# Two-expert routed layer: the routed experts' second product with the weights stationary, and three moves around it

## The reference, cut to what matters

```python
x = L0_attn_x                                   # (4, 1024, 128) float32
xn = _layernorm(x)
s = attention(xn)                               # 16 heads of 8, elu+1, rope, softmax, plus a 3-tap convolution of v
g = _silu(ffn(xn))
x = x + s * g

def ffn(u):
    h_s = experts_mlp(u, g_shared, W1_s, b1_s, W2_s, b2_s).sum(axis=-2)        # 2 shared experts, 128 -> 512 -> 128
    scores = jax.nn.sigmoid(u @ centroids)                                      # 8 routed experts
    gpk, i_topk = jax.lax.top_k(scores, 2)
    gk = gpk / scores.sum(axis=-1, keepdims=True)
    routed_all = experts_mlp(u, g_routed, W1_r, b1_r, W2_r, b2_r)
    h_r = (gk[..., None] * take(routed_all, i_topk)).sum(axis=-2)
    return u + h_s + h_r
# experts_mlp: gelu(rmsnorm(u) @ W1 + b1) @ W2 + b2
```

## Time and profile before

| | |
|---|---|
| median of 3 runs | 1197.69 us (1197.49 to 1198.04) |
| the profiled execution | 1197.96 us |
| its span, first to last instruction | 1195.8 us |
| mean granted TensorE clock | 0.983 |
| TensorE (PE) busy | 1151.4 us, 96% |
| TensorE weight loads (PEld) | 696.4 us, 58% |
| VectorE (DVE) busy | 832.6 us, 70% |
| ScalarE (ACT) busy | 753.3 us, 63% |
| GpSimd (POOL) busy | 393.0 us, 33% |

### The profile page before, as it was taken

How to read it: one execution, slowest core, us unless ns; L and a number is a source line. 1 busy time by engine, 2 the same in 40 slices (tenths; PEclk the granted TensorE clock), 3 DMA queues, 4 the chain that set the end, 5 groups by cost and what they waited for, 6 DMA issues and landing times.

```text
span 1195.8 us, 17687 instructions
## 1 busy us (share of the span) xinstructions
PE 1151.4 (96%) x6212; PEld 696.4 (58%) x6212; DVE 832.6 (70%) x1562; ACT 753.3 (63%) x1393; POOL 393.0 (33%) x436
## 2 busy tenths in 40 slices
PE   5999999799989999999999999999999999999996
PEld 4666679799965545555555555555555555545542
DVE  6723243255538888887888888788888878888870
ACT  5454455444546666766666667666666676766676
POOL 0166653300025371441506153251515234142000
PEclk9799999899999999999999999999999999999998
DMA  9011145554431202021120202112020202112000
GB/s 339 10 52 45 45 128 158 139 151 144 147 88 43 79 6 59 15 77 36 39 61 5 58 15 76 29 44 62 8 58 15 76 11 58 46 28 56 4 7 5
DMA packets 73864, 75.32 MB, mean 63 GB/s; under 512 B 25248, under 2 KB 58912, under 8 KB 73264
## 3 DMA queue, kind: packets, MB, share of 16 engines
q1 hardware_dynamic: 69680, 65.80, 20.0%
q0 software_dynamic: 4096, 8.40, 2.4%
HBM read 30.06 MB, written 18.35 MB: 40 GB/s over the span
## 4 chain that ended last, share of the span: by engine, by line
PE 63%; DVE 6%; issue 1%; ACT 0%; POOLq 0%; POOL 0%; DVEq 0%; ACTq 0%
PE ps L1431 22%; PE ps L1443 20%; PE ps L1088 18%; DVE neg_half L1155 4%; PE ps L1109 1%; DVE acc L1502 1%; PE ps L1117 1%; PE ps L1114 0%; DVE pre L1184 0%; PE ps L1102 0%; ACT prob L1471 0%; DVE pv_sb L1507 0%; DVE attn L1198 0%; DVE r_sum L1193 0%; ACT L1471 0%
## 5 line engine op out<-in xcount | busy, mean ns | idle before, releaser
L1155 DVE TENSOR_REDUCE neg_half<-ps 128x1 f32<-128x512 f32 x1024 | 647.2, 684 | 178.4 <-PE ps L1088 168.6
L1471 ACT ACTIVATE prob<-ps 128x512 f32<-128x512 f32 x1024 | 545.1, 598 | 210.9 <-PE ps L1431 190.6
L1431 PE MATMUL ps<-q_raw,k_mask 128*128 128x512 f32 x1024 | 431.4, 426 | 4.4 <-ACTq L1464 3.9
L1088 PE MATMUL ps<-k_raw,q_mask 128*128 128x512 f32 x1024 | 412.9, 403 | 9.1 <-DMA q_mask<-raw 6.3
L1431 PEld LDWEIGHTS ps<-q_raw,k_mask 128*128 128x128 f32 x1024 | 191.7, 188 | 231.8 <-ACT prob L1471 160.8
L1443 PE MATMUL ps<-prob,v_st 128*32 128x512 f32 x2048 | 272.7, 604 | 2.5 <-issue 1.2
L1088 PEld LDWEIGHTS ps<-k_raw,q_mask 128*128 128x128 f32 x1024 | 193.6, 189 | 50.7 <-DVE neg_half L1155 14.6
L629 ACT ACTIVATE hidden<-ps,w 128x512 f32<-128x512 f32 x92 | 62.9, 688 | 83.9 <-PE ps L513 77.5
L1385 POOL TENSOR_TENSOR result<-attn,acc 128x256 f32<-128x256 f32 x16 | 11.8, 736 | 294.6 <-DVE attn L1198 158.0
L534 PEld LDWEIGHTS ps<-w,hidden 128*128 128x128 f32 x736 | 95.4, 193 | 6.2
L534 PE MATMUL ps<-w,hidden 128*128 128x128 f32 x736 | 97.5, 276 | 0.0
(11 more groups left out here) (152 smaller groups left out, 1018.4 us busy)
## 6 DMA issues: line engine op xcount, KB each, us to landing
w<-in_w SPq DMA_DIRECT2D x23, 322.0 KB, 4.0
k_mask<-k_raw SPq DMA_DIRECT2D x64, 96.0 KB
slots<-zero SPq DMA_DIRECT2D x4, 1472.0 KB, 11.6
w_raw<-in_w SPq DMA_DIRECT2D x23, 256.0 KB, 2.9
x_tok<-slots SPq DMA_DIRECT2D x23, 256.0 KB, 3.3
answers<-y_tok SPq DMA_DIRECT2D x23, 256.0 KB, 2.3
k_raw<-raw SPq DMA_DIRECT2D x16, 256.0 KB
q_mask<-raw SPq DMA_DIRECT2D x64, 64.0 KB
```

Of the source, the lines that this page charges most:

```text
L1088: nc.tensor.matmul(max_bank(par, k, lone_bank)[:, :], q_mask[par][:, j, qt * P:(qt + 1) * P], k_raw[par][:, kh * CH:(kh + 1) * CH], start= ...
L1155: nc.vector.tensor_reduce(out=neg_half[par][:, qt, j, kh:kh + 1], in_=max_bank(par, k, lone_bank)[:, :], axis=AX.X, op=ALU.max, negate=True)\
L1431: nc.tensor.matmul(score_bank(n, par, s)[:, :], k_mask[par][:, j, kt * P:(kt + 1) * P], q_raw[par][:, qh * CH:(qh + 1) * CH], start=True, ...
L1471: nc.scalar.activation(prob[s // J % 2][:, j, :], score_bank(n, par, s)[:, :], ACT.Exp, scale=SCALE)\
```

## The change

The routed blocks' `down` takes the form of the shared ones: w2 stationary, the hidden tile moving, one product of 512 columns a step. Each routed block's sums are then copied by ScalarE (into the first four tiles of `xr_all`, free by then), transposed back by `stand` in step 3 of the next block, and taken by VectorE's `output`, which moves from step 2 to step 3. For the last block, copy, transposes and output come at the end of the stage. `FIRST_MAX` goes from 9 to 10. The two `y_tok` tiles become the halves of `x_b`, which is now reserved from the start; the wait for the last stores moves from the end of the stage to the third one, on SyncE ahead of the load of `x_b` and on GpSimd ahead of the first gather. ScalarE does one exponential of a single column at the end of the stage.

```diff
-        y_tok = [sb(f"y_tok{i}", [P, CT, C]) for i in range(SPARE)]
+        y_tok = ffn["y_tok"]
         b2_sum = sb("b2_sum", [P, C])
+        warm = sb("warm", [P, 1])
...
+        def lying_of(u):
+
+            return (lying if u < SHARED else ffn["xr_all"][:, 0:CT, :].rearrange("p t c -> p (t c)"))
...
                 ahead.sync(sp, k)
-            for i in range(SPARE):
-                sp.wait_ge(y_st[i], 16 * ((ROUTED + SPARE - 1 - i) // SPARE))
...
                 pe.wait_ge(gelu_ok, n + 1)
-                if u < SHARED:
-                    nc.tensor.matmul(bank[:, :], w2, hidden[n % HB][:, :], start=q == 0, stop=q == of(u) - 1)\
-                      .then_inc(down_ok, 1)
-                    return
-                for t in range(CT):
-                    last = nc.tensor.matmul(bank[:, t * P:(t + 1) * P], hidden[n % HB][:, t * P:(t + 1) * P], w2,
-                                            start=q == 0 and t == 0, stop=q == of(u) - 1, skip_group_check=True)
-                last.then_inc(down_ok, 1)
+                nc.tensor.matmul(bank[:, :], w2, hidden[n % HB][:, :], start=q == 0, stop=q == of(u) - 1)\
+                  .then_inc(down_ok, 1)
...
-                    if 1 <= u <= SHARED and q == LAG + 1:
+                    if 1 <= u and q == LAG + 1:
                         stand(u - 1)
...
+            stand(UNITS - 1)
...
+            def lay_down(u):
+                act.wait_ge(down_ok, hids_before(u + 1))
+                if u > 0:
+                    act.wait_ge(stood_full, u)
+                nc.scalar.activation(lying_of(u), y_ps[u % 2][:, :], ACT.Copy).then_inc(lying_ok, 1)
...
-                if 1 <= u <= SHARED and q == LAG:
-                    act.wait_ge(down_ok, hids_before(u))
-                    if u > 1:
-                        act.wait_ge(stood_full, u - 1)
-                    nc.scalar.activation(lying[:, :], y_ps[(u - 1) % 2][:, :], ACT.Copy).then_inc(lying_ok, 1)
+                if 1 <= u and q == LAG:
+                    lay_down(u - 1)
...
+            lay_down(UNITS - 1)
+            nc.scalar.activation(warm[:, :], ffn["gain_r"][:, :], ACT.Exp).then_inc(warm_ok, 1)
+            act.wait_ge(warm_ok, 1)
...
             def output(u):
-                if u < SHARED:
-                    dve.wait_ge(stood_full, u + 1)
-                else:
-                    dve.wait_ge(down_ok, hids_before(u + 1))
+                dve.wait_ge(stood_full, u + 1)
...
-                if q == (LAG if u > SHARED else LAG + 1) and u > 0:
+                if q == LAG + 1 and u > 0:
                     output(u - 1)
...
-        FIRST_MAX = 9
+        FIRST_MAX = 10
...
+        def answers_stored(eng):
+
+            for i in range(2):
+                eng.wait_ge(answer_st[i], 16 * ((ROUTED + 1 - i) // 2))
...
+            answers_stored(sp)
             sp.dma_start(x_b[:, :, :], x_v[0, :, :, :]).then_inc(x_b_in, 16)
...
                 if n == 0:
+                    answers_stored(pool)
                     gather(0, 0, KT * TOPK)
...
+            ffn["y_tok"] = [tiles["x_b"][:, i * CT:(i + 1) * CT, :] for i in range(2)]
+            ffn["y_st"] = tiles["answer_st"]
```

More of the change, by code:

```diff
@@ L376, in experts @@
         y_out = sem("f_y_out")
-        y_st = [sem(f"f_y_st{i}") for i in range(SPARE)]
+        y_st = ffn["y_st"]
         v_full = sem("f_v_full")
+        warm_ok = sem("f_warm_ok")
         rest_full = sem("f_rest_full")
@@ L541, in stand @@
                 for t in range(CT):
-                    last = nc.tensor.transpose(y_ps[u % 2][:, t * P:(t + 1) * P], lying[:, t * P:(t + 1) * P],
+                    last = nc.tensor.transpose(y_ps[u % 2][:, t * P:(t + 1) * P], lying_of(u)[:, t * P:(t + 1) * P],
                                                ident[:, :])
@@ L862, in attention @@
         neg_max = sb("neg_max", [P, KT, J, 1])
+        x_b = sb("x_b", [P, KT, C])
         s_ps = psum[0:SB]
@@ L867, in attention @@
         first_round_ps, first_max_ps = psum[6], psum[7]
+        answer_st = [sem(f"a_answer_st{i}") for i in range(2)]
         w_in = sem("a_w_in")
@@ L1282, in attention @@
         tiles = {"k_mask": k_mask[0], "q_mask": q_mask[0], "stage": stage, "rope": rope, "feat": feat, "pre": pre,
-                 "v_st": v_st}
+                 "v_st": v_st, "x_b": x_b, "answer_st": answer_st}
         first_stages(Ahead, tiles)
@@ L1294, in attention @@
         picked = [sb(f"picked{i}", [P, KT, C]) for i in range(TOPK)]
-        x_b = sb("x_b", [P, KT, C])
         tanh_b = sb("tanh_b", [P, KT, C])
```

## The result

| | before | after |
|---|---|---|
| median of 20 runs | 1197.49 us (1196.18 to 1198.08) | 1199.89 us (1198.37 to 1202.73) |
| ratio | | 1.0023, 95% interval 1.0017 to 1.0029 |
| profiled execution | 1197.96 us | 1199.31 us |
| its span | 1195.8 us | 1197.1 us |
| TensorE busy | 1151.4 us | 1153.6 us |

The change makes the kernel 2.4 us slower. That lies at the edge of what the forecast called the same (up to 1200.1 us), 0.9 us above the value that it gave. Profile against profile, the change is +1.35 us. TensorE's busy time grows by 2.2 us: about 6 us of work are new, and about 3 us that the slower clock added to the products behind the old hole are gone.

The account below looks back on a forecast made before the run. TensorE, busy for all of the routed stage, was taken as the bound. The terms −3.7 + 9.9 + 0.9 + 0.3 − 9.3 + 4.5 + 0.2 − 1.5 gave +1.3 us, hence 1199.0 us, range 1195.0 to 1203.0.

Parts of the forecast that it names:

- the old hole: Kernel before, routed block 9, step 0: first maximum waits 6.28 us for q_mask's rows; with slow clock 9.3 us.
- Part 1: Routed second product with w2 stationary: exposed part of six weight loads saved, 0.04 us in 92 steps, −3.7 us.
- rival C: Routed second product: the removed weight loads were exposed, about 1128 us; chance 0.01.
- Part 2: Transposes back in routed blocks: 22 more calls on TensorE at 0.45 us each, +9.9 us.
- Part 3: ScalarE's copy in routed blocks: hidden in plain blocks, +0.9 us in block 4, +0.3 us in block 8.
- step (8, 3): Routed block 8, step 3: ScalarE comes late from an exponential, put at +0.3 us.
- Part 4: First maximum a block later: −9.3 us for hole and slow clock, +4.5 in block 10, +0.2 in block 11.
- Part 5: Answers' tiles under x's tile, store waits moved to the third stage: nothing on TensorE waits, 0 us.
- Part 6: End of stage: longer chain, earlier barrier (−0.5), table load (up to −2.0), clock (+1.0): −1.5 us.
- Rival A: Block 10: nothing behind the row moves is late, x_tok lands in time, faster, 1193.5 us; chance 0.21.
- Rival B: Block 10, step 1: the hole moves there and keeps its slow clock, slower, 1202.7 us; chance 0.27.
- Rival D: End of stage: the barrier still waits for the last store, 1201.3 us; chance 0.03.

Follow-up runs that it names:

- run 10: Changed kernel with the row moves spread over SyncE's steps 8, 9 and 10, without copy and transposes of the routed blocks: 1182.31 us, ratio 0.9880.
- run 8: Changed kernel with the old second product and the row moves spread over SyncE's steps 8, 9 and 10: 1186.44 us, ratio 0.9905.
- run 3: Changed kernel with the routed second product as before (w2 moving, no copy, no transposes, output in step 2): 1190.62 us, ratio 0.9940.
- run 5: Kernel before with only the new end of the stage (answers' tiles, moved store waits, table load ahead of the barrier): 1194.77 us, ratio 0.9977.
- run 1: Changed kernel with the first maximum put back from block 10 to block 9: 1204.53 us, ratio 1.0059.
- run 7: Changed kernel with the ten row moves spread over SyncE's steps 8, 9 and 10 instead of all in step 10: 1196.01 us, ratio 0.9987.
- run 2: Kernel before with only the first maximum moved to block 10: 1194.75 us, ratio 0.9977.
- Run 6: Kernel before with only the exponential's table load put ahead of the barrier: 1197.47 us, ratio 0.9995.
- run 4: Changed kernel without copy and transposes of the routed blocks, row moves not spread: 1188.58 us, ratio 0.9917.
- 9: Changed kernel with the row moves spread and each routed block's four transposes done twice: 1203.98 us, ratio 1.0058.

## Why the prediction was right, step by step

- **Part 1, −3.7 us for w2 stationary.** Right: −4.1 (run 10 against run 8). The weight loads lay under the products: 92 steps with fewer of them gave 4.1 us, and rival C with its 1128 us is out. That one price of 0.04 us served for all steps is partly luck: a plain step gave 0.03 (1.59 to 1.56), a step with a maximum about 0.06. The rule of the Trainium skill weighed beside it (TensorE: Matmul & The Clock Gate, Part 3, The mechanism) is not borne out by these runs: 4.1 us instead of an estimated 59. The same section also lets a load go ahead of running products when it fills the background weight buffer, which the prediction left out. The runs fit that, since eight loads a step take 1.09 us and nearly all of it lies under the products; which buffer they fill no run shows.
- **Part 2, +9.9 us for the transposes.** Right: 0.44 a block in the timeline, 9.7 in 22 blocks. Together with part 1, the copy, its waits and the longer chain at the end the new form costs 9.3 us (run 3 against the changed kernel), 9.8 (run 5 against run 1) and 9.6 (run 8 against run 7), three pairs with different surroundings. The prediction's terms for the same are 9.9 − 3.7 + 0.9 + 0.3 + 1.5 = 8.9. What is missing lies in the waits: turning back costs 13.7 us (run 7 against run 10) where the terms make 9.9 + 0.9 + 0.3 + 1.5 = 12.6.
- **Part 3, ScalarE's copy.** Hidden in plain blocks as said. Exposed in block 4 for 7.76 − 7.13 = 0.63 us (block starts at 190.52 and 198.28) instead of 0.9, and in step (8, 3) for 0.4 instead of 0.3 (2.42 us, from 227.41 to 229.83, against 2.01).
- **Part 4, −9.3 + 4.5 + 0.2 for the first maximum.** −4.6 in sum, and run 1 measured 4.6. The mechanism is right, the match of the sums is partly luck. Block 10 lost 12.12 − 8.04 = 4.1 us against the 4.5 forecast: the hole was 3.18 us instead of 2.6, since x_tok took 4.3 us to land instead of 3.3, and in the profiled execution the clock did not fall (I had counted 1.0). The 1.8 us idle after which the clock was said to fall in the old hole were read from the edge of a stretch; cut finer, the clock is 1.00 up to about 230.4, 2.0 us into the hole. Block 11 lost 258.23 − 249.06 − 8.04 = 1.1 us instead of 0.2 (block 11 starts at 249.06, an undisturbed block with maxima takes 8.04 us). The term that was too small is that last one: two gelus wait 7.06 and 5.03 us for w_2, and the second wait makes ScalarE's copy late in block 11. Its cause is not the one in the prediction either: run 7 spreads the row moves and block 11 still loses 1.2 us, with w_2 issued behind the moves of `place_score_rows`. By the profile the part is −9.3 + 4.1 + 1.1 = −4.1 us. In the kernel before, the same move brought only 2.7 (run 2).
- **Part 5, nothing for the moved waits.** Right: nothing on TensorE waited for x_b or the gathers.
- **Part 6, −1.5 us at the end.** −0.96 in the profile (8.29 against 9.25). The barrier's part is right: the first score comes 350.74 − 347.43 = 3.31 us after the last product instead of 3.92, 0.6 less (forecast 0.5), and the barrier opens 0.8 us behind the output (350.30), as forecast. The mis-sized term is "up to −2.0" for the table load, with 1.0 taken back by the clock: from the first score to the first weighing it is 4.98 us instead of 5.33, −0.35 where −1.0 was forecast. Run 6 has the table load at 0.36 us in the profile and at nothing in the median, because TensorE's first products ran at the slower clock and would have taken nearly as long without it. Most of the gain of the end is the landing of the last store.
- **The sum.** The medians moved by +2.4 us where +1.3 was forecast. By the runs, the end gave 2.7 (run 5), the new form cost 9.8 (run 1 against run 5) and the first maximum gave 4.6 (run 1); the terms for them were 3.0, 8.9 and 4.6. In this order nearly all of the miss is in the new form. In the order of runs 2 and 3 it is in the first maximum, 2.7 instead of 4.6, and 4.1 at the end and 9.3 for the new form make up for a part of it. The parts overlap, so the miss has no single place.
- **Rival A** fell at its own condition (x_tok was issued 8.1 us behind the first row move, not under 5.5); with 3.8 us in run 7 the hole is gone, as it had it. **Rival B** did not occur in the profile, but the runs of the changed kernel reach 1202.73 us, B's value, and the four above 1201.5 have the lowest mean clock of all 20 (0.982). Run 4's profile shows the same hole with a clock of 0.56 behind it. So the slower clock in some of the runs is likely behind those four. It does not order the others: four runs at 0.995 took 1200.2 to 1200.9 us, the nine at 0.986 to 0.989 took 1198.4 to 1201.1. No run here isolates it. **Rival D** did not occur: the first score comes 1.93 us after the last output starts.

## What to carry to other kernels

A second product turned around costs its transposes back where TensorE is the bound: here 0.44 us a block against 0.14 to 0.23 saved in four steps, however few weight loads are left. When an in-order DMA queue carries a burst of small moves, what counts is what stands behind the burst. Moving the consumer of the burst passed a smaller hole on (2.7 to 4.6 us gained), while spreading the burst over three steps removed that hole as well (another 3.9 to 4.2 us). Before pricing a hidden latency such as a table load, ask what else holds the same stretch back, here TensorE at the slower clock.

## What the runs showed of the hardware that was not expected

- Whether the clock falls after a hole is not a matter of its length alone. It stayed at full speed through holes of 3.18 us (changed kernel) and 2.06 us (run 8). It fell 3.0 us into the hole of 3.88 us (run 4), 2.0 us into the one of 6.28 (before), and at the end of the same 2.06 us in run 3, where the average was 0.58 over the next 4 us. In run 7 it was still 1.00 when TensorE resumed at the barrier and fell about 1.4 us later.
- Nine profiles have a hole of 1.97 to 2.06 us ahead of the first score (the changed kernel and runs 1, 3, 4, 5, 7, 8, 9 and 10). In five the clock fell there (the changed kernel, 1, 3, 5, 7), in four it did not (4, 8, 9, 10). A fall costs 4.96 − 3.70 = 1.3 us: the time from the first score to the first weighing in runs 3 (342.99 to 347.95) and 8 (339.05 to 342.75), which run the same code there. A comparison of two single profiles can be off by as much.
- A DMA of one size and kind (x_tok, 256 KB) landed 3.3 us after its issue in the median, and 4.3 us behind a burst of row moves.
